# Image-and-text block on one NeuronCore: the scan input carries its factor of 16 from the start, a new slot plan, and 24 more idle matmuls in the first stage

## What is computed

```
y  = layernorm(patches16x16(x)) * ln1_g + ln1_b ; y = y @ W + bias ; y = layernorm(y) * ln2_g + ln2_b
h  = concat(y (32 x 196 x 256), txt (32 x 77 x 256))                  # 273 tokens
xs = rmsnorm(layernorm(h)[:, ::2]) * g_norm                           # every second token: 137 steps
x_proj, gate = split(xs @ w_in.T + b_in)
for each step:  s = tanh(s * A + x_t[:, :, None] * Bm) ; y_t = s @ sum(Cm) + Dv * x_t     # s: 32 x 256 x 64
h  = h + repeat((y * silu(gate)) @ w_out.T + b_out, 2)
h  = h + (silu(z @ wg.T) * (z @ wu.T)) @ wd.T, z = layernorm(h)       # integer weights / 127, hidden size 768
```

## Time and profile before

| what | value |
|---|---|
| median of 3 runs | 1288.39 us (1287.45 to 1291.64) |
| the profiled execution's own time | 1288.43 us |
| its span, first to last instruction | 1286.7 us |
| mean granted PE clock, share of full speed | 0.982 |

### The profile page before, as it was taken

One profiled execution on the slowest core, in us unless ns is written; L12 is line 12 of the kernel. 1 busy time (PEld: TensorE's weight loads), 2 busy tenths in 40 slices (PEclk: granted clock), 3 DMA queues, 4 the chain that ended last, 5 costly groups with the idle time before them and its releaser, 6 DMA issues.

```text
span 1286.7 us, 26087 instructions
## 1 busy us (share of the span) xinstructions
PE 1193.1 (93%) x7217; PEld 643.8 (50%) x7217; DVE 1078.1 (84%) x2423; ACT 982.7 (76%) x1944; POOL 434.3 (34%) x435
## 2 busy tenths in 40 slices
PE   6788999999999999999999999999999999999987
PEld 4543546464646464646464646464444444444435
DVE  4898988898989898989898989878989889888843
ACT  2358796979797979797979797978888787787852
POOL 6522252525252525252525252514132121321320
PEclk8879899999999999999999999999999999999989
DMA  7423233232323232323232323222322323322210
GB/s 168 129 50 87 58 83 76 71 88 68 89 70 87 71 86 70 87 71 85 70 87 71 85 72 85 65 50 67 93 73 78 96 61 85 85 73 65 66 50 23
DMA packets 154815, 99.60 MB, mean 77 GB/s; under 512 B 129073, under 2 KB 143537, under 8 KB 153425
## 3 DMA queue, kind: packets, MB, share of 16 engines
q1 hardware_dynamic: 151120, 97.58, 29.8%
q10 hardware_dynamic: 3648, 1.46, 0.5%
HBM read 58.39 MB, written 40.60 MB: 77 GB/s over the span
## 4 chain that ended last, share of the span: by engine, by line
PE 46%; DVE 16%; issue 14%; ACT 11%; DMA 5%; POOL 3%; SPq 2%; DVEq 1%; ACTq 0%; POOLq 0%
PE Y L1394 11%; PE U L1384 9%; DVE U L829 7%; PE P L1460 7%; ACT h L1097 5%; PE P L1564 5%; PE P L1565 4%; DMA raw<-in_x 3%; PE P L1580 2%; PE P L1581 2%; PE P L1443 2%; PE P L1495 2%; DMA y_scr<-y_fx 1%; PE P L1515 1%; ACT fsg L1201 1%
## 5 line engine op out<-in xcount | busy, mean ns | idle before, releaser
L829 DVE TENSOR_TENSOR U<-h,a_col 128x512 f32<-128x512 f32 x1096 | 708.2, 689 | 85.6 <-ACT h L1097 81.1
L1097 ACT ACTIVATE h<-U 128x512 f32<-128x512 f32 x1096 | 611.1, 609 | 155.6 <-PE U L1384 150.5
L1384 PE MATMUL U<-x_diag,b_st 128*128 128x512 f16 x1096 | 368.7, 383 | 42.6 <-DVE U L829 40.1
L1394 PE MATMUL Y<-h,read_st 128*32 128x512 f32 x2192 | 266.8, 605 | 5.9 <-ACT h L1097 5.9
L1384 PEld LDWEIGHTS U<-x_diag,b_st 128*128 128x128 f16 x1096 | 101.3, 98 | 210.9 <-DVE U L829 153.5
L1313 POOL TENSOR_TENSOR xT_act<-act,xT_act 128x448 f16<-128x448 f32 x114 | 117.9, 1038 | 157.0 <-ACT xT_act L1206 157.0
L1460 PE MATMUL P<-tok_w,xT_act 128*112 128x256 f32 x648 | 160.6, 381 | 0.1
L1460 PEld LDWEIGHTS P<-tok_w,xT_act 128*112 128x112 f32 x648 | 113.1, 177 | 41.4 <-ACT xT_act L1121 10.1
L1394 PEld LDWEIGHTS Y<-h,read_st 128*32 128x32 f32 x2192 | 57.5, 109 | 134.2 <-issue 106.4
L1580 PE MATMUL P<-down_w,xT_act 128*112 128x256 bf16 (+1 forms) x480 | 114.6, 275 | 2.3 <-DVE xT_act L1006 1.6
L1581 PE MATMUL P<-down_w,xT_act 128*112 128x256 bf16 (+1 forms) x480 | 114.4, 275 | 0.0
(11 more groups left out here) (165 smaller groups left out, 1514.3 us busy)
## 6 DMA issues: line engine op xcount, KB each, us to landing
raw<-in_x SPq DMA_DIRECT2D x42, 448.0 KB, 6.2
gate_scr<-gate_o SPq DMA_DIRECT2D x20, 448.0 KB, 2.5
gate_in<-gate_scr SPq DMA_DIRECT2D x20, 448.0 KB, 7.8
tok_scr<-tok SPq DMA_DIRECT2D x19, 448.0 KB, 3.2
res<-tok_scr SPq DMA_DIRECT2D x19, 448.0 KB, 3.7
out<-res SPq DMA_DIRECT2D x76, 112.0 KB, 2.3
x_diag<-scan_scr SPq DMA_DIRECT2D x312, 16.0 KB
x_diag<-scan_scr SPq DMA_DIRECT2D x304, 12.0 KB
```

The costliest lines, as they stand in the source:

```text
L829: dve.tensor_tensor(U[bank_of(slot)][:, :].rearrange("p (l b) -> p l b", b=B), h[:, (slot - CHUNKS) % RING, :].rearrange("p (l b) -> p l b ...
L1097: sc.activation(h[:, slot % RING, :], U[bank_of(slot)][:, :], ACT.Tanh, scale=1.0 / U_SCALE).then_inc(squashed, 1)
L1384: pe.matmul(U[bank_of(slot)][:, :], b_st[:, c, :], x_diag[:, c, :, t * B:t * B + B], start=False, stop=True, skip_group_check=True).then_i ...
L1394: mm = pe.matmul(Y[c4 * 32:c4 * 32 + 32, :], read_st[:, t, half, :], h[:, (t * CHUNKS + half * RG + c4) % RING, :], start=(t == 0 and half ...
```

## The change

xf holds 16 x: the bias and the factor are applied in one ACT instruction, a new DVE piece `col_scale` prepares 16 b_in and Dv/16 once, the high half is a plain copy and the low half a plain subtraction. The slots of almost all pieces are new, and so is POOL's order. In the first stage a new piece `warm` issues 24 matmuls (three times `FILL` = 8) whose result is not used, behind the last `embed` and ahead of `turn_xa`. Cut to what is spoken of:

```
 "image":
-        read=(0, 12, 18, 29, 33, 42, 51), shrink=(2, 2, 4, 5, 6, 6, 8, 8), turn=(8, 9, 10, 10, 11, 12, 13, 16),
-        attend=(16, 16), average=(18, 20), embed=(18, 19, 19, 20, 21, 22, 24, 24, 26, 27, 28, 28), turn_fx=(31,
-        32), ffn_gate=(35, 36, 39, 40, 47, 53), ffn_up=(35, 39, 42, 46, 51, 53), turn_xa=(38,), project=(40, 41,
-        47, 48), finish=(8, 11), ...
-        fx_low_part=(35, 35), ... x_low_part=(45,), ffn_product=(38, 41, 46, 47, 53, 55),
-        xT_copy=(8, 8, 8, 10, 10, 12, 12, 17), ... tok_normalise=(27, 38), x_copy=(41,),
-        act_high_part=(36, 46, 48, 50, 53, 55), normalise=(28, 28, 28, 29, 42, 47, 49) ...
+        read=(0, 10, 18, 29, 32, 44, 51), shrink=(3, 3, 3, 3, 4, 5, 5, 5), turn=(5, 6, 7, 7, 8, 9, 10, 13),
+        attend=(14, 14), average=(18, 20), embed=(16, 16, 18, 19, 20, 21, 22, 25, 25, 25, 27, 27), turn_fx=(31,
+        31), ffn_gate=(34, 36, 40, 42, 47, 52), ffn_up=(34, 39, 43, 45, 51, 53), turn_xa=(36,), project=(41, 41,
+        47, 49), finish=(5, 8), ...
+        fx_low_part=(34, 34), ... x_low_part=(44,), ffn_product=(37, 41, 45, 48, 53, 55),
+        xT_copy=(5, 6, 6, 6, 8, 10, 10, 13), ... tok_normalise=(27, 39), x_copy=(40,),
+        act_high_part=(44, 47, 50, 51, 55, 55), normalise=(25, 29, 42, 45, 47, 48, 50) ...
 "first":
-        turn=(0, 0, 0, 0, 0, 2, 4, 5), embed=(0, 4, 6, 8, 11, 12, 12, 12, 13, 13, 16, 17), weight_turn=(0, 0, 0, 0),
-        turn_xa=(24,), project=(25, 39, 42, 50), average=(27, 40), b_split=(0, 0, 1, 3, 6, 8), clear_stage=(11,),
-        raw_patch=(11, 11, 16, 16, 24, 25, 29, 31, 33, 34, 35, 37, 38, 38), raw_means=(42,), diag_half=(49,) ...
+        warm=(34, 34, 34), col_scale=(2,), turn=(0, 1, 3, 10, 16, 16, 18, 21),
+        embed=(13, 15, 17, 22, 23, 25, 25, 25, 28, 28, 29, 33), weight_turn=(1, 2, 4, 11),
+        turn_xa=(35,), project=(38, 40, 43, 48), average=(37, 43), b_split=(0, 0, 0, 1, 1, 3), clear_stage=(46,),
+        raw_patch=(3, 6, 8, 9, 9, 10, 10, 16, 17, 18, 26, 28, 35, 37), raw_means=(39,), diag_half=(41,) ...
 POOL_ORDER["image"]:
-        gating, res_rsqrt, raw_rsqrt, token_rsqrt 0, token_tiles 0, ln_rsqrt, token_rsqrt 1, normalise 0, token_tiles 1,
-        normalise 1, normalise 2, act_low_part 0, act_low_part 1, normalise 3, 4, act_low_part 2, skip_term, ...
+        gating, res_rsqrt, raw_rsqrt, token_rsqrt 0, token_tiles 0, ln_rsqrt, token_rsqrt 1, token_tiles 1, normalise 0,
+        act_low_part 0, normalise 1, normalise 2, skip_term, normalise 3, 4, act_low_part 1, ...
+        def col_scale(dve):
+            dve.wait_ge(s_cols, 48)
+            dve.tensor_scalar(cols[:, 0:DB], cols[:, 0:DB], X_SCALE, None, ALU.mult).then_inc(s_scaled, 1)
+            dve.tensor_scalar(cols[:, 4:4 + DB], cols[:, 4:4 + DB], 1.0 / X_SCALE, None, ALU.mult).then_inc(s_scaled, 1)
+        def warm(pe):
+            pe.wait_ge(s_zero, 1)
+            pe.wait_ge(s_ev, 1)
+            idle = h[:, 0, :].bitcast(FP16)
+            for _ in range(FILL):
+                pe.matmul(U[0][:, :], idle[:, 0:128], idle[:, 0:CW], start=True, stop=True)
-                dve.scalar_tensor_tensor(x_lo[:, :, :], xf[:, :, :], X_SCALE, x_hi[:, :, :], ALU.mult, ALU.subtract)\
-                    .then_inc(x_lo_done, 1)
+                dve.tensor_tensor(x_lo[:, :, :], xf[:, :, :], x_hi[:, :, :], ALU.subtract).then_inc(x_lo_done, 1)
 x_copy:
+                if not due(g):
+                    sc.wait_ge(s_scaled, 2)
-                                  ACT.Identity, bias=cols[:, k:k + 1]).then_inc(xf_done, 1)
+                                  ACT.Identity, scale=X_SCALE, bias=cols[:, k:k + 1]).then_inc(xf_done, 1)
-                sc.activation(x_hi[:, :, :], xf[:, :, :], ACT.Copy, scale=X_SCALE).then_inc(x_hi_done, 1)
+                sc.activation(x_hi[:, :, :], xf[:, :, :], ACT.Copy).then_inc(x_hi_done, 1)
```

More of the change, by code:

```diff
@@ L72 @@
[L72 to L76, removed]
@@ L77 @@
-    "text": dict(
[L78 to L83, removed]
+        read=(0, 10, 18, 29, 32, 44, 51), shrink=(3, 3, 3, 3, 4, 5, 5, 5), turn=(5, 6, 7, 7, 8, 9, 10, 13),
@@ L84 @@
         residual=(32,)),
     "last": dict(
[L86 to L90, removed]
@@ L91 @@
-    "first": dict(
[L92 to L100, removed]
@@ L101 @@
-    "second": dict(
[L102 to L109, removed]
-        bias_split=(0, 0, 1, 4, 4, 8, 36, 38, 39)),
@@ new lines @@
+        ffn_gate=(36, 44, 46, 47, 49, 55), ffn_up=(39, 44, 46, 47, 49, 55), finish=(13, 19), res_stats=(41,),
+        res_variance=(42,), res_shift=(42,), fx_low_part=(43, 47), ffn_product=(47, 48, 51, 54, 55, 55),
+        y_copy=(2,), fx_apply=(33, 33, 34, 41), fxT_copy=(42, 43), ffn_silu=(45, 45, 47, 48, 52, 54),
+        act_high_part=(47, 47, 49, 52, 54, 55), residual=(35,), y_next=(45,)),
+    "first": dict(
+        warm=(34, 34, 34), col_scale=(2,), turn=(0, 1, 3, 10, 16, 16, 18, 21), embed=(13, 15, 17, 22, 23, 25, 25, 25, 28, 28, 29,
+        33), weight_turn=(1, 2, 4, 11), weight_copy=(0, 8, 12, 18), xT_copy=(6, 10, 14, 15), first_copy=(0, 0,
+        2, 2), tok_stats=(11, 41), tok_centre=(18, 19), tok_affine=(19, 25), tok_shift=(51,),
+        tok_normalise=(26,), ln_stats=(27,), ln_shift=(38,), ln_apply=(15,), ln_apply_first=(41,),
+        turn_xa=(35,), xaT_copy=(16,), project=(38, 40, 43, 48), x_copy=(23,), x_low_part=(53,),
+        gate_silu=(34,), raw_patch=(3, 6, 8, 9, 9, 10, 10, 16, 17, 18, 26, 28, 35, 37), raw_means=(39,),
+        average=(37, 43), raw_deviation=(43,), raw_variance=(47,), raw_shift=(55,), normalise=(36, 40, 41, 46,
+        51, 52, 55), clear_banks=(51,), sum_c=(48,), read_scale=(55,), b_split=(0, 0, 0, 1, 1, 3), c_pair=(2,),
+        clear_stage=(46,), diag_half=(41,), keep_busy=(52, 54, 55)),
@@ L121 @@
+        average=(1, 1), bias_part=(39, 42, 49, 51, 51, 55), normalise=(0, 2, 4, 8, 12), bias_add=(55,),
         keep_busy=(0, 0, 4)),
@@ L1024, in vector_body @@
                     bias_add(dve)
+                for k in parts_at(plan, "col_scale", slot):
+                    col_scale(dve)
                 for k in parts_at(plan, "c_pair", slot):
```

65 lines of the change are left out of this document (44 added, 21 removed).

## The result

The changed kernel takes **1310.61 us** (1310.22 to 1311.24, 4 runs) against 1288.99 for the kernel before in the same session (1287.45 to 1291.64, 4 runs): ratio 1.0166, 95% interval 1.0148 to 1.0184. The forecast was 1282.8, its range ended at 1293. It is slower by 21.6 us, on the side that had a chance of 0.19, and far beyond that rival's price.

A forecast was written before the change was run, and what follows sets the result against it. PE, busy 93% of the span, was taken as the bound, its idle time in image stages as all a new order can win. 1288.43 us less 4.6 (x path) and 1.0 (head) gave 1282.8, range 1275 to 1293.

The forecast's parts named there:

- The arithmetic, 0: Low half and ACT's factor: plain subtraction as long as the old form and still held by POOL; worth 0.
- The x path, -4.6 us: Image stages 2 to 12: low half 1.3 us, PE's wait 0.4 us shorter each; -4.6 us, bounds 0 and -9.7.
- The rest of the image stages: Earlier shrinks and transposes: PE's other shrinks hide DVE's wait; taken 0, bounds -0.3 and +0.5 us a stage.
- `fx_low` moved one slot: Image stages: one `grow` earlier, but copies start later; between -0.3 and +0.3 us, taken 0.
- The head, -1.0 us: First stage: 24 matmuls keep the clock full; xf 1.0 us earlier, bounds -2.2 and +1.
- Text stages: Boundary order kept, low half not held: 0, bounds 0.2 us each either way over six.
- the slower one: Image-stage front: bunched shrinks make DVE wait, transposes paced by ACT's copies; 0.5 us a stage, 1294 us, chance 0.19.

The follow-up runs named there:

- run 1: Kernel before with its slots and POOL order, only the arithmetic changed, no idle matmuls: 1289.56 us, ratio 1.0004.
- run 9: Kernel before, old arithmetic and head, only the first feed-forward chunk's high half moved from slot 36 to 44 in image stages: 1279.52 us, ratio 0.992.
- run 8: Kernel before's image, text and last plans with changed arithmetic, first and second stages, idle matmuls; first high half in slot 44: 1276.99 us, ratio 0.9906.
- run 11: Kernel before's plans with changed arithmetic, no idle matmuls, first feed-forward chunk's high half in slot 44: 1277.88 us, ratio 0.9905.
- run 13: Changed kernel in all its slots, image stages' pixel transfers cut from 448 KB to 28 KB each: 1286.96 us, ratio 0.9971.
- run 12: Run 8 with the image stages' pixel statistics and means in the changed kernel's early slots: 1345.92 us, ratio 1.0416.
- run 3: Changed kernel with only the image stages' pixel statistics and means back in their old slots: 1310.99 us, ratio 1.0162.
- run 4: Changed kernel with 7 idle matmuls ahead of the second transposes in image stages from 3 on: 1307.29 us, ratio 1.0140.
- run 10: Run 8 without the 24 idle matmuls behind the first group's embedding: 1277.41 us, ratio 0.9897.
- run 5: Changed kernel with the whole image-stage plan and POOL's order there taken from the kernel before: 1292.58 us, ratio 1.0019.
- run 7: Changed kernel with text and last stages' plans and POOL's order there taken from the kernel before: 1308.81 us, ratio 1.0151.
- run 6: Changed kernel with only the later half of the image-stage plan, POOL's order included, from the kernel before: 1322.38 us, ratio 1.0263.

## Why the prediction was wrong, step by step

- **The arithmetic, 0**: right. 1289.56 against 1289.5 us in run 1, and the plain subtraction is held like the old form, 1.89 us against 0.62 in the text stages. The rule of the Trainium skill that the prediction cites (SBUF — State Buffer, Who interferes with whom) counts `tensor_tensor` with two SBUF inputs among the instructions that contend with GpSimd's reads, and these two figures agree with it.
- **The x path, -4.6 us**: the low half came near, 1.21 us against 1.3, though 1.3 was only the middle between two ends. It met the second token instruction as forecast, with 0.73 us of it left, and ended 0.48 behind it; the pixel instruction that followed on POOL took 0.92 us instead of 0.55, so this time POOL waited and not DVE. The size of the gain was too small. I let PE's 0.88 us shrink in proportion to the low half. It goes as a whole: in the nine stages 4 to 12 of after PE waits 8.7 us on `grow` in 9 times, the one at the stage's end, where before it waited 16.1 us in 18. Run 9 measures it alone: 10.0 us, near the 9.7 of the bound; runs 8 and 11, with the arithmetic and in 8 the head changed too, have 13.1 and 11.7. PE needs that `grow` only at a certain moment; once it is ready by then, nothing of the wait is left.
- **The rest of the image stages, 0, bounds -0.3 and +0.5 us a stage**: this is the step that failed. It is +1.9 us a stage over the whole (stages 3 to 12), and +2.8 when the x path's gain of 0.88 is put beside it. "PE has the other four `shrink` to do meanwhile, which hides it" was right for `finish` 0: DVE waits 1.55 us there and PE doesn't. But I counted PE, DVE and ACT and never SP: `raw_patch` was moved from slot 9 to slot 6 and I named no price for it. The trace of before had the answer: issue at 447.07, first statistic at 455.76, a distance of 8.7 us where the last transfer had landed after 8.65. They landed just in time, with less than 0.2 us to spare in any of the stages 3 to 12; in two of these (4 and 9) DVE already waited 0.2 us for them. In slot 6 the statistic comes 4.6 us behind `y_copy` (run 13), and the pixels land 5.8 us behind it, since the later half of the new plan also issues them 0.9 us later (2.75 us ahead of `y_copy` instead of 3.66). The price is 1.05 to 1.9 us of DVE's standing on the pixels in each of the stages 3 to 12 of after, and behind it 1.6 to 2.4 us of PE's at `finish` 1. Runs 12 and 13 show this mechanism from both sides. Run 3 adds that the landing is not the only way to lose there: with the statistics late enough for it, the early transposes cost as much.
- **The clock in the image stages**: not in the prediction; "at full clock" stood as a fact of the stage. It is the second part of the loss, 1.7 us in each of five stages (run 4: 3.3 us back in the medians when PE is kept busy).
- **`fx_low` moved one slot, between -0.3 and +0.3, taken 0**: +0.67 us a stage (6.1 us in nine stages of run 13, 1.9 in all of before, none of it in an image stage). Which of the moves there does it was not tested alone. That and 0.2 at `finish` are what eats the x path's 0.88 in run 13, where the stage is 64.27 as before.
- **The head, -1.0 us**: the clock part came true, full from 24 to 54 us and `project` 1 done 0.8 us earlier. The size is not shown: the loads of the first scan are 0.1 us earlier, and the -1.13 at the first `y_copy` is the difference of two single profiles in a spread of 2.8 us. Nothing of it reaches the end in runs 8, 10 and 11.
- **Text stages, 0, bounds 0.2**: +0.42 each, outside the bounds (runs 5 and 7); the slot behind it is open.
- **The rivals**: the slower one had the place nearly right, the waits at `finish` 1 and the transposes, and the cause wrong: it blamed the shrinks, and priced it at 0.5 us a stage. With the shrinks as bunched and the pixels there in time (run 13) the wait is 0.44 us. Its sum was wrong as well: 1288.4 and 5.5 and 1.0 are 1294.9, not 1294. And of the "seven transposes ahead of `read` 1" the trace of after shows six.

A version that beats both kernels came out of this: run 8, 1276.99 us, the old slots with one of the new ones. Most of it, 10.0 of 13.1 us, is run 9's single number.

## What to carry to other kernels

Before a consumer is moved forward, read for every operand when it was issued and when it landed, and compare that with when it was used: a wait of zero in the trace can be a margin of less than 0.2 us. Instructions behind the wait in the same queue are part of its price, and so is what the matrix engine's clock does after it has stood. A plan of some fifty slots is one object; taking one verified move out of a new plan and putting it into the old one was worth 10 us, while the whole new plan lost 22, and the old image plan with its front half new lost 32 (run 6).
